# A mixture-of-experts stage: when row slots are freed, how the products of two-expert tiles are laid out, and how the last tile's result leaves

## The reference

```python
B, L, D, H, E = (8, 4096, 256, 1024, 8)     # here D = 256, H = 1024, E = 8, TOP_K = 2
gate_logits = xf @ Wg + bg
top_w, top_i = jax.lax.top_k(gate_logits, TOP_K)
top_w = jax.nn.softmax(top_w, axis=-1)
w_dense = jnp.sum(jax.nn.one_hot(top_i, E, dtype=xf.dtype) * top_w[..., None], axis=1)
out = jnp.zeros_like(xf)
for e in range(E):
    h = jax.nn.gelu(xf @ W1[e] + b1[e], approximate=False)
    out = out + w_dense[:, e:e + 1] * (h @ W2[e] + b2[e])
```

## Time and profile before

| what | value |
|---|---|
| median of 3 runs | 1247.88 us (1243.93 to 1252.08) |
| the profiled execution | 1247.95 us, its span 1246.1 us |
| PE busy | 1096.8 us (88%) |
| DVE, ACT, POOL busy | 759.0, 743.1, 731.0 us |
| mean granted PE clock | 0.95 of full speed |
| stage e, first transpose to end | 613.8 to 1246.1 us |

### The profile page before, as it was taken

How to read it: one execution, slowest core, us unless ns; L and a number is a source line. 1 busy time by engine, 2 the same in 40 slices (tenths; PEclk the granted TensorE clock), 3 DMA queues, 4 the chain that set the end, 5 groups by cost and what they waited for, 6 DMA issues and landing times. The chain is left out here.

```text
span 1246.1 us, 37906 instructions
## 1 busy us (share of the span) xinstructions
PE 1096.8 (88%) x12025; PEld 953.0 (76%) x12026; DVE 759.0 (61%) x2691; ACT 743.1 (60%) x1771; POOL 731.0 (59%) x786
## 2 busy tenths in 40 slices
PE   4998888999999879972299999999999999998994
PEld 2666678999999868862178888888888888887783
DVE  7887787998989849976144444444444444443341
ACT  3556577898989847753155555555555555555541
POOL 7323255676666616777446666666666666665454
PEclk9999898999999989976599999999999999999998
DMA  7889788788788559997212322323323232323122
GB/s 180 235 253 272 226 225 206 195 205 195 193 202 202 161 187 352 370 311 246 91 15 48 52 49 47 52 43 52 49 49 51 43 52 48 52 48 46 33 41 26
DMA packets 150570, 168.43 MB, mean 135 GB/s; under 512 B 15694, under 2 KB 141694, under 8 KB 150086
## 3 DMA queue, kind: packets, MB, share of 16 engines
q1 hardware_dynamic: 109270, 123.59, 34.8%
q0 software_dynamic: 21984, 31.18, 14.3%
q10 hardware_dynamic: 19232, 12.64, 4.7%
HBM read 107.52 MB, written 64.70 MB: 138 GB/s over the span
## 5 line engine op out<-in xcount | busy, mean ns | idle before, releaser
L1698 ACT ACTIVATE e_g_hi<-e_ps_h,keep_b 128x256 f16<-128x256 f32 x392 | 203.0, 518 | 247.5 <-PE e_ps_h L1601 247.4
L1764 DVE TENSOR_TENSOR e_g_lo<-e_gf,e_g_hi 128x256 f16<-128x256 f32 x424 | 184.2, 434 | 161.4 <-ACT e_gf L1698 139.6
L1635 PE MATMUL e_ps_y<-w2s,e_g_hi 128*128 x1696 | 282.1, 273 | 0.0
L1601 PE MATMUL e_ps_h<-e_xt,w1s 128*128 128x256 f16 x2352 | 269.4, 275 | 4.8 <-PEq L1593 4.3
L1601 PEld LDWEIGHTS e_ps_h<-e_xt,w1s 128*128 x2352 | 224.4, 98 | 43.8 <-issue 10.3
L977 POOL TENSOR_TENSOR b_p<-b_s,b_p 128x392 f16<-128x392 f32 x196 | 178.9, 934 | 96.3 <-DVE b_p L864 82.7
L1635 PE MATMUL e_ps_y<-w2s,e_g_lo 128*128 x848 | 231.8, 273 | 0.0
L1553 POOL DMA_INDIRECT out<-e_y,e_xg x106 | 176.3, 1663 | 84.0 <-POOLq L1548 41.1
L1698 ACT ACTIVATE e_gf<-e_ps_h,keep_b 128x256 f32<-128x256 f32 x392 | 205.5, 524 | 0.0
L1635 PEld LDWEIGHTS e_ps_y<-w2s,e_g_hi 128*128 128x128 f16 x1696 | 164.3, 98 | 18.6
L923 ACT ACTIVATE b_s<-b_s,b_neg_max 128x196 f32<-128x196 f32 x392 | 158.9, 458 | 0.3 <-DVE b_neg_max L845 0.2
(11 more groups left out here) (175 smaller groups left out, 1666.2 us busy)
## 6 DMA issues: line engine op xcount, KB each, us to landing
h_v<-v_rows SPq DMA_DIRECT2D x196, 99.5 KB
e_xg<-slots SPq DMA_DIRECT2D x49, 273.0 KB, 2.7
a_w_in<-in_w SPq DMA_DIRECT2D x16, 512.0 KB, 4.8
c_w_in<-in_w SPq DMA_DIRECT2D x16, 512.0 KB, 9.3
v_rows<-h_v_sb SPq DMA_DIRECT2D x14, 455.0 KB, 7.1
a_x<-in_x SPq DMA_DIRECT2D x14, 448.0 KB, 6.6
qk_hi<-h_o_hi SPq DMA_DIRECT2D x14, 448.0 KB, 4.8
qk_lo<-h_o_lo SPq DMA_DIRECT2D x14, 448.0 KB, 5.7
```

Source lines behind the costliest of these rows:

```text
L1601: mm = pe.matmul(ps_h[:, hc % 4, 0:ST], w1s[:, bass.ds(e, 1), w, a:a + 128].rearrange("p a n -> p (a n)"), xt[:, s, :, 2 * p + k, :], star ...
L1635: mm = pe.matmul(ps_y[:, s, h * C:(h + 1) * C], g[:, s, hc, h * 128:(h + 1) * 128], w2s[:, bass.ds(experts[h], 1), w, a:a + C].rearrange(" ...
L1698: last = act.activation(dst, ps_h[:, hc % 4, 0:ST], ACT.Gelu, bias=b1_sb[:, bass.ds(e * HC + hc, 1)], scale=1.0 / WSCALE)
L1764: dve.tensor_tensor(g_lo[:, s, hc, :], gf[:, hc % 4, :], g_hi[:, s, hc, :], ALU.subtract).then_inc(gs_ok, 1)
```

## The change

It has three parts. (1) On POOL the wait for the earlier scatters and the release of the slot leave `send` and become `landed(n)`, which stands at the head of the turn, ahead of `weigh(n+2)`. (2) For two-expert tiles `up_halves(m)` and `down(m-1)` are merged: after each of the 8 chunks of 12 short products come 6 long ones of the tile before, and `turn(m+1)` comes after the fourth chunk. The merged form waits at its start for all 8 splits of tile m-1. DVE's `take_x` goes between the fourth and the fifth split to match. (3) The last tile's result goes through the free `ps_h` buffers, half by half: `take_y_by_halves` on DVE and `send_by_halves` on POOL, where the wait for earlier scatters comes after the gate product of the first half.

```diff
+                def landed(n):
+                    pool.wait_ge(y_done, 32 * n)
+                    pool.sem_inc(xg_free, 1)
+                def scatter(j, h):
+                    pool.indirect_dma_start(out=out, out_offset=bass.IndirectOffsetOnAxis(
+                        ap=xg[:, j, h, TAIL:TAIL + 1], axis=0), in_=y_sb[:, j % 2, h, :], in_offset=None,
+                        compute_op=ALU.add).then_inc(y_done, 16)
...
                 def send(j, n, apart=False):
 
                     s = j % 2
                     pool.wait_ge(yf_ok, 1)
                     pool.sem_inc(yf_ok, -1)
-                    if n is not None:
-                        pool.wait_ge(y_done, 32 * n)
-                        pool.sem_inc(xg_free, 1)
                     for h in range(2):
                         last = pool.tensor_scalar(y_sb[:, s, h, :], y_f[:, s, h, :], gate[:, j, h:h + 1], None, ALU.mult)
                     last.then_inc(y_out, 1)
...
-                        pool.indirect_dma_start(out=out, out_offset=bass.IndirectOffsetOnAxis(
-                            ap=xg[:, j, h, TAIL:TAIL + 1], axis=0), in_=y_sb[:, s, h, :], in_offset=None,
-                            compute_op=ALU.add).then_inc(y_done, 16)
+                        scatter(j, h)
+                def send_by_halves(j, n):
+                    for h in range(2):
+                        pool.wait_ge(yf_ok, h + 1)
+                        pool.tensor_scalar(y_sb[:, j % 2, h, :], y_f[:, j % 2, h, :], gate[:, j, h:h + 1], None, ALU.mult
+                                           ).then_inc(y_out, 1)
+                        pool.wait_ge(y_out, h + 1)
+                        if h == 0:
+                            pool.wait_ge(y_done, 32 * n)
+                        scatter(j, h)
...
                 for j in range(U):
+                    if j:
+                        landed(j)
                     weigh((j + 2) % U)
-                    send(j, j if j else None)
+                    send(j, j)
                 with pool.Fori(1, LOOPED // U) as i:
                     for j in range(U):
+                        landed(U * i + j)
                         weigh((j + 2) % U)
                         send(j, U * i + j)
                 for n in range(LOOPED, NT):
+                    if n + 1 < NT:
+                        landed(n)
                     if n + 2 < NT:
                         weigh((n + 2) % U)
-                    send(n % U, n, n in halves)
+                    if n + 1 < NT:
+                        send(n % U, n, n in halves)
+                    else:
+                        send_by_halves(n % U, n)
...
+                def down(m, s, experts, first=0, last=6 * HC):
+                    for i in range(first, last):
+                        h, n = i // (3 * HC), i % (3 * HC)
+                        hc, (g, w) = n // 3, ((g_hi, 0), (g_hi, 1), (g_lo, 0))[n % 3]
+                        a = hc * C
+                        mm = pe.matmul(result(m == NT - 1, s, h), g[:, s, hc, h * 128:(h + 1) * 128],
+                                       w2s[:, bass.ds(experts[h], 1), w, a:a + C].rearrange("p a n -> p (a n)"),
+                                       start=n == 0, stop=n == 3 * HC - 1)
+                        if n == 3 * HC - 1 and (h or m == NT - 1):
+                            mm.then_inc(y_ok, 1)
...
+                def up_halves(m, experts, now):
 
                     s = m % 2
                     pe.wait_ge(xt_ok, 1)
                     pe.sem_inc(xt_ok, -1)
+                    pe.wait_ge(gs_ok, HC)
                     for hc in range(HC):
-                        pe.wait_ge(gs_ok, hc - 3 + HC)
+                        if hc >= 4:
+                            pe.wait_ge(gs_ok, hc - 3 + HC)
...
                         mm.then_inc(h_ok, 1)
+                        down(m - 1, (m - 1) % 2, now, 6 * hc, 6 * hc + 6)
+                        if hc == 3:
+                            turn(m + 1)
                     pe.sem_inc(gs_ok, -HC)
```

The rest of the diff takes `down` out of its old place, passes the experts along on PE, and on DVE:

```diff
+                def take_y_by_halves(n):
+                    e = dve.value_load(tile_expert[0:1, n:n + 1], min_val=0, max_val=E - 1)
+                    dve.wait_ge(y_free, 1)
+                    for h in range(2):
+                        dve.wait_ge(y_ok, h + 1)
+                        dve.scalar_tensor_tensor(y_f[:, n % 2, h], result(True, n % 2, h), 1.0 / WSCALE,
+                                                 b2_sb[:, bass.ds(e, 1), :].rearrange("p a c -> p (a c)"), ALU.mult, ALU.add
+                                                 ).then_inc(yf_ok, 1)
...
+                    if n + 1 in halves:
+                        split((n + 1) % 2, 0, 4)
+                        take_x((n + 2) % U, n + 2, n + 2 in halves)
+                        split((n + 1) % 2, 4, HC)
+                    elif n + 1 < NT:
+                        split((n + 1) % 2)
+                        if n + 2 < NT:
+                            take_x((n + 2) % U, n + 2, n + 2 in halves)
                     if n + 1 < NT:
-                        split((n + 1) % 2)
-                    if n + 2 < NT:
-                        take_x((n + 2) % U, n + 2, n + 2 in halves)
-                    take_y(n % U, n, False, n in halves)
+                        take_y(n % U, n, False, n in halves)
+                    else:
+                        take_y_by_halves(n)
```

More of the change, by code:

```diff
@@ L1468, in stage_e, with result @@
         xg_f = xg[:, :, :, :].bitcast(F32)
+        def result(ends, s, h):
+            return ps_h[:, h, 0:C] if ends else ps_y[:, s, h * C:(h + 1) * C]
         xg_in = [sem(f"e_xg_in{i}") for i in range(U)]
@@ L1607, in up @@
                         pe.sem_inc(gs_ok, -HC)
-                def up_halves(m, experts):
+                def down(m, s, experts, first=0, last=6 * HC):
[9 more added lines that the diff above has]
+                def up_halves(m, experts, now):
                     s = m % 2
@@ L1655, in _ @@
                         turn(j + 2)
-                        down(j, (e, e))
+                        down(None, j % 2, (e, e))
                         e = after
@@ L1663, in _ @@
                         pe.wait_ge(gs_ok, HC)
+                        down(n, n % 2, now)
                     elif n + 1 in halves:
                         u = 2 * (n + 1 - PAIR0)
-                        up_halves(n + 1, (expert_of_half(u), expert_of_half(u + 1)))
                         after = (expert_of_half(u), expert_of_half(u + 1))
+                        up_halves(n + 1, after, now)
+                        now = after
                     else:
                         e = expert(n + 1)
-                        after = (e, e)
                         up(n + 1, e, False)
-                    if n + 2 < NT:
-                        turn(n + 2)
-                    down(n, now)
-                    now = after
+                        if n + 2 < NT:
+                            turn(n + 2)
+                        down(n, n % 2, now)
+                        now = (e, e)
             @block.scalar
@@ L1759, in take_x, with split @@
                     last.then_inc(gap_ok, 1)
-                def split(s):
-                    for hc in range(HC):
+                def split(s, first=0, last=HC):
+                    for hc in range(first, last):
                         dve.wait_ge(g_ok, hc + 1)
@@ L1765, in split @@
                                           ).then_inc(gs_ok, 1)
-                    dve.sem_inc(g_ok, -HC)
+                    if last == HC:
+                        dve.sem_inc(g_ok, -HC)
                 def take_y(j, n, begins, apart=False):
```

## The result

The changed kernel takes 1287.09 us (median of 4 runs, 1283.64 to 1289.15), the kernel before in 4 runs 1249.45. The ratio is 1.030 with a 95% interval of 1.026 to 1.035. The forecast was 1265 us with a range to 1276. The way is the forecast one; the size is not.

The account below looks back on a forecast made before the run. PE bounds the loop before, at 10.95 us; POOL's chain then sets 11.60. Tile 50's second scatter at 1241.4 plus 22.1 for the end gives a 1263.5 us span; with 1.85 around it, 1265 us, range 1250 to 1276.

Parts of the forecast that it names:

- The wait at the head makes POOL's turn a closed chain: In the expert loop, POOL's operations follow the last scatter's landing; POOL's 11.60 us beat replaces PE's 10.95.
- `weigh`, 2.44 us: In POOL's loop turn, the four small operations take 2.44 us from first start to last end.
- rival C: In the loop, DVE and POOL disturb each other more: beat 11.9 us, 1280 us; chance 0.06 together with Rival D.
- B: In the loop, the chain exists but is shorter: beat 11.2 to 11.45 us, 1245 to 1258 us; chance 0.15.
- Rival A: In the loop, POOL's beat stays under PE's 10.95 us, so the kernel gets faster: 1231 us; chance 0.12.
- The extras: On POOL's chain up to tile 50: three late second scatters add 7.0 us, four two-expert tiles' waits 9.0 us.
- The end: From tile 50's second scatter to the span's end: 22.1 us, with 2.7 us of gate product and hand-over off the path.
- The gain of the merged products lies off the path: In two-expert tiles, PE gains 12.7 us, but its 13.0 us a tile stays under POOL's 13.85.
- The merged tile: Two-expert tile on PE: 11.6 us with chunks of 1.4 us and transposes, plus 1.4 us of stall, 13.0 us.
- the two rows that I had: Bounds for a merged chunk on PE: short products at 56 ns give 1.33 us, at 85 ns 1.67 us.
- The hole at the head: Ahead of a merged tile, PE waits 1.4 us for all splits of the tile before; table reads hide in it.
- Rival D: PE's new stalls bring a lower clock, changing little and only at the end; chance 0.06 together with rival C.

Follow-up runs that it names:

- small splits: The changed kernel with DVE's splits writing only 2 of 256 columns: 1288.98 us, ratio 1.010 to the kernel before on the same chip.
- the wait at the head alone: The kernel before with only the wait for earlier scatters and the slot release moved ahead of `weigh`: 1322.63 us, ratio 1.039.
- parts 2 and 3 alone: The changed kernel with the wait and release put back in `send`, behind the wait for the result: 1265.84 us, ratio 0.993 to the kernel before.
- the wait behind `weigh`: The changed kernel with the wait and release moved between `weigh` and `send`: 1259.99 us, ratio 0.989 to the kernel before.

## Why the prediction was right in kind and wrong in size

**The wait at the head makes POOL's turn a closed chain, and POOL's beat becomes the loop's: right.** The chain was read link by link from the rows; here it is with what came out (us, means over 37 turns of the loop, tiles 2 to 44 without the three late second scatters and the turns behind them):

| link | forecast | before | changed | small splits |
|---|---|---|---|---|
| second scatter to `weigh` | 4.05 | 2.57 | 4.06 | 4.07 |
| `weigh` | 2.44 | 2.44 | 2.65 | 2.45 |
| to the gate products | 0.30 | 1.07 | 0.31 | 0.31 |
| gate products | 1.97 | 2.03 | 2.03 | 1.84 |
| to the first scatter | 0.89 | 0.94 | 0.94 | 0.94 |
| to the second | 1.95 | 1.99 | 1.96 | 1.95 |
| beat | 11.60 | 11.04 | 11.94 | 11.55 |

**The mis-sized term: `weigh`, 2.44 us.** I took it from the earlier trace rows, where it runs while DVE waits for the result and touches nothing. Before, it starts 0.19 us after DVE has written the gaps, in nearly every turn; behind the landing it starts 3.0 to 8.7 us after them, when DVE is at the splits. Its last operation in the loop before (count: ns min/median/max), to be held against the two of the experiment with small splits:

```profile
L1532 POOL TENSOR_TENSOR e_gate<-e_ex,e_invert x43: 707/708/712, 649.8 to 1115.2; 128x2 f32<-128x2 f32 x43
```

The timeline of DVE of the changed kernel in the turn that is shown above:

```profile
1111.29 0.43 DVE L1797 TENSOR_TENSOR e_g_lo<-e_gf,e_g_hi 128x256 f16<-128x256 f32 x1 [0.93 <-ACT e_gf L1731]
1112.02 0.42 DVE L1797 TENSOR_TENSOR e_g_lo<-e_gf,e_g_hi 128x256 f16<-128x256 f32 x1 [0.30 <-ACT e_gf L1731]
1112.76 0.42 DVE L1797 TENSOR_TENSOR e_g_lo<-e_gf,e_g_hi 128x256 f16<-128x256 f32 x1 [0.31 <-ACT e_gf L1731]
```

The split at 1111.29 lies on the third operation of `weigh` (1111.45, 0.36 us instead of 0.25), the next two on the fourth (1112.07, 0.94 instead of 0.71). It is so in the whole loop: the third operation takes 0.25 us in each of the 11 turns where DVE does nothing beside it, and 0.32 in the mean of the 29 where a split lies on it. With small splits `weigh` is back at 2.45: that is shown, not argued. It is 0.21 of the 0.34 us that the beat was short; the other 0.13 are the gate products (0.06) and the first scatter, which comes late now and then (0.05), means of links of which I had taken single rows. Multiplied by 50 turns the 0.34 us are 17 us. That is most of the 22 us between 1265 and 1287; another 3.5 are the median over the profiled execution, which I had taken as equal. I had this as rival C, a beat of 11.9, and gave it 0.06, because the longest gate product was 1.19 us. That bounded the wrong operation: in the loop of the trace before, a split touches `weigh` in one turn of 43, so its rows could show nothing of this, and the range ought to have carried it. (Two slips in the rivals change none of this: B's lower end is 50 x 0.4 = 20 us below the forecast and not 15, as its 1245 has it, and by a chunk of 1.63 us A would end at 1238 and not 1241.)

**The extras: right.** The three late second scatters added 7.6 us (forecast 7.0), the two-expert tiles' own wait 9.4 (9.0). From tile 0's second scatter (644.90) to tile 50's (1259.19) are 50 x 11.94 + 17.0 = 614.0 us; the trace has 614.3, the forecast 596.0.

**The end: right.** POOL of the changed kernel at the end, tile 52:

```profile
1268.93 1.51 POOL L1570 TENSOR_SCALAR e_y<-e_y_f,e_gate 128x256 f32<-128x256 f32 x1
1272.40 1.60 POOL L1546 DMA_INDIRECT out<-e_y,e_xg  x1 [1.95 <-DMA out<-e_y,e_xg]
1273.48 1.50 POOL L1570 TENSOR_SCALAR e_y<-e_y_f,e_gate 128x256 f32<-128x256 f32 x1
1276.58 1.60 POOL L1546 DMA_INDIRECT out<-e_y,e_xg  x1 [1.59 <-issue]
```

(The first row's 1.51 us and the third's 1.50 overlap others in the record.) The second scatter comes 4.18 us behind the first, where the forecast had 4.21. From tile 50's second scatter to the end of the span 22.6 us, forecast 22.1.

**"The gain of the merged products lies off the path": wrong.** It is worth 6.9 us even with the wait at the head (62.1 against 55.2 us). The merged tiles stay just under POOL's chain, 14.1 us against 11.94 + 2.35 = 14.3, but I had let a PE of 15.5 us a tile pass on the argument that it finishes early enough on the whole. It doesn't: it is 1.2 us a tile over POOL's chain, which uses up the 2.8 us that it had to spare in two to three tiles (an estimate from these numbers), and with the wait at the head alone POOL waits 2.1 to 2.5 us for the result in three of these turns.

**The merged tile: 13.0 us forecast, 14.1 measured.** Tile 47 of the changed kernel on PE:

```profile
1181.46 1.14 PE L1663 MATMUL e_ps_h<-e_xt,w1s 128*128 128x128 f16 x12 [1.23 <-DVE e_g_lo L1797]
...
1183.30 0.97 PE L1663 MATMUL e_ps_h<-e_xt,w1s 128*128 128x128 f16 x12
...
1187.90 0.61 PE L1613 MATMUL e_ps_x<-keep_id,e_xg 128*128 128x128 f16 x8
1188.34 0.83 PE L1663 MATMUL e_ps_h<-e_xt,w1s 128*128 128x128 f16 x12
...
1195.70 1.15 PE L1663 MATMUL e_ps_h<-e_xt,w1s 128*128 128x128 f16 x12 [1.33 <-PEq L1653]
```

The chunks begin 1.3 to 1.9 us apart, where I took 1.4 and bounded it by 1.67. The mean of tile 47's seven distances is 1.61 us, with the transposes in one; without these 0.45 us it is 1.54. In tile 46 it is 1.47. So the chunk lies between the two rows that I had, and not at either. The rows tell how: the short products of one chunk follow each other at (1.14 - 0.23) / 11 = 83 ns in the first, (0.97 - 0.22) / 11 = 68 in the second and (0.83 - 0.22) / 11 = 55 in the fifth, right behind the transposes. Inside the second, start by start, the first eight come 56 ns apart and the last four 60 to 124. It looks as if PE's sequencer had eight of them ready from the time of the long products and then fell back to its own pace; that wasn't tested. By "TensorE: Matmul & The Clock Gate" of the Trainium skill, section on the back-to-back issue gap, such products come about 81 ns apart in a stream with weight loads. The trace agrees for the 96 products in a row of the kernel before, (8.20 - 0.22) / 95 = 84 ns, and doesn't for the merged tiles, whose chunks have 60 to 67 ns in the mean. Tile 47 without the hole at its head takes 12.9 us, where I had 11.6. The hole at the head, 1.33 us ahead of tile 48, is as large as forecast (1.4), but it is the table reads' and not, as I had it, the wait for all splits: with the wait taken chunk by chunk it is still 1.28. The wait for the splits ends only the first hole, 1.23 us ahead of tile 47.

**Rival A** (the beat stays PE's) falls by the links; its price for a kernel without the chain, 1231 us or 1.4% less than before, was too good as well: parts 2 and 3 alone give 0.7%, with the wait behind `weigh` 1.1%. **Rival D** (clock): the granted clock fell to half (1.2 GHz) three times in the changed loop, at 739.9, 920.8 and 1101.7 us, and not once in that stretch before. The three falls go with PE's three long waits at the transposes, 3.27, 3.23 and 3.31 us, which end at 738.8, 920.1 and 1101.9 us, behind the late second scatters. The turns of POOL in which the clock was low took 11.83, 12.02 and 11.87 us, no longer than the mean of 11.94, so it isn't what the forecast lacked.

What stays open is why the fourth operation of `weigh` suffers more from a split than the second (a median of 0.77 instead of 0.71 us, where the second stays at 0.72), and what makes the second scatter late in every 15th tile.

## What to carry to other kernels

An engine with idle time is free only in the order in which it stands: a wait moved ahead of work that used to pass under it closes a chain, and the sum of that chain has to be held against the beat of the bounding engine before the wait is moved. Put the wait behind the last work that doesn't need it; here its place before or after four small operations decides between 3.9% slower and 0.3% faster. And price a moved operation for what will run beside it at its new place, since a row from the old place shows only its old neighbours.

## What the runs showed of the hardware

GpSimd's small operations, 128 x 2 numbers, take longer beside VectorE's 128 x 256 subtractions: one of 0.71 us takes 0.77 in the median and 0.95 at most, one of 0.25 up to 0.44; with the subtractions cut to two columns they are at 0.71 and 0.25 again (0.73 and 0.26 at most). An accumulating scatter of 128 rows to DRAM takes 3.8 us in the median from issue to landing in the changed loop (3.7 to 4.3) and with small splits, 3.9 in the loop before, of which GpSimd is held 1.55 to 1.65. And 128-column products, each with weights of its own whose address comes from a register, ran 84 ns apart in a row of 96, but 56 ns apart in a row of 12 right behind the transposes; six long products between every twelve brought the mean inside the chunks of a tile to 60 to 67 ns.
